# A selective-scan block on one Trainium2 core: GpSimd's products, sums and skip terms made two channel blocks at a time

## What is computed

```python
def step(h, inp):
    xt, dtt, bt, ct = inp
    dA = jnp.exp(A[None] * dtt[..., None])
    dB = dtt[..., None] * bt[:, None, :]
    h = dA * h + dB * xt[..., None]
    y = jnp.sum(h * ct[:, None, :], axis=-1)
    return (h, y)
...
xz = x @ w_in.T + b_in
x_ssm, z = jnp.split(xz, 2, axis=-1)
z = jax.nn.silu(z)
dt = jax.nn.softplus(x_ssm @ w_dt.T + b_dt)
Bm = x_ssm @ w_B.T + b_B
Cm = x_ssm @ w_C.T + b_C
y = _selective_scan(x_ssm, dt, A, Bm, Cm)
y = y + D[None, None, :] * x_ssm
y = y * z
y = y @ w_out.T + b_out
```

## Time and profile before

| what | value |
|---|---|
| time, median of 3 runs | 4594.26 us (4590.93 to 4594.27) |
| span of the profiled execution | 4588.9 us, 5.4 us less than that median |
| PE, busy | 4344.2 us, 95% |
| POOL, busy | 4161.1 us, 91% |
| ACT, busy | 3817.6 us, 83% |
| DVE, busy | 3679.8 us, 80% |
| POOL's products (L364), 2048 of 128 x 512 | 2590.8 us |
| POOL's sums (L375), 512 of 128 x 512 | 653.4 us |
| mean granted TensorE clock | 0.991 |

### The profile page before, as it was taken

One profiled execution on the slowest core, in us unless ns is written; L12 is line 12 of the kernel. 1 busy time (PEld: TensorE's weight loads), 2 busy tenths in 40 slices (PEclk: granted clock), 3 DMA queues, 4 the chain that ended last, 5 costly groups with the idle time before them and its releaser, 6 DMA issues. The chain is left out here.

```text
span 4588.9 us, 71982 instructions
## 1 busy us (share of the span) xinstructions
PE 4344.2 (95%) x22528; PEld 2805.6 (61%) x22528; DVE 3679.8 (80%) x5132; ACT 3817.6 (83%) x6371; POOL 4161.1 (91%) x3343
## 2 busy tenths in 40 slices
PE   7999999999999999999999999999999999999997
PEld 3666666666666666666666666666666666666664
DVE  3778888888887888888888888888878888888885
ACT  3788888888888888888888888888888888888885
POOL 3899999999999999999999999999999999999995
PEclk8999999999999999999999999999999999999999
DMA  3111111111111111111121111111111111111111
GB/s 129 45 43 58 58 58 45 56 51 57 60 58 48 49 59 59 58 46 54 51 62 59 59 44 56 51 57 60 54 45 54 60 61 58 47 53 51 58 49 39
DMA packets 140915, 254.79 MB, mean 56 GB/s; under 512 B 18597, under 2 KB 18597, under 8 KB 140538
## 3 DMA queue, kind: packets, MB, share of 16 engines
q1 hardware_dynamic: 140538, 250.19, 17.2%
HBM read 215.50 MB, written 34.63 MB: 55 GB/s over the span
## 5 line engine op out<-in xcount | busy, mean ns | idle before, releaser
L364 POOL TENSOR_TENSOR work<-work,c_bc 128x512 f32<-128x512 f32 x2048 | 2590.8, 1280 | 266.6 <-DVE work L1127 180.9
L1127 DVE TENSOR_TENSOR_SCAN work<-work,state,b_ps 128x512 f32<-128x512 f32 x1792 | 2250.5, 1273 | 351.9 <-PE b_ps L453 343.2
L839 ACT ACTIVATE work<-u_td,b_td 128x512 f32<-128x512 f32 x2048 | 1455.4, 711 | 147.5 <-PE b_ps L453 142.2
L829 ACT ACTIVATE work<-dt_t,neg_a 128x512 f32<-128x512 f32 x2048 | 1454.1, 710 | 12.5 <-DVE work L1127 12.1
L453 PE MATMUL b_ps<-ident,work 128*128 128x128 f32 x8192 | 1246.2, 275 | 67.2 <-DVE work L1127 57.0
L453 PEld LDWEIGHTS b_ps<-ident,work 128*128 128x128 f32 x8192 | 966.7, 142 | 344.5 <-issue 173.4
L530 PEld LDWEIGHTS y_ps<-ident,work 128*128 128x128 f32 x6144 | 758.4, 142 | 635.7 <-issue 586.5
L530 PE MATMUL y_ps<-ident,work 128*128 128x128 f32 x6144 | 916.2, 274 | 4.7 <-POOL work L375 3.5
L375 POOL TENSOR_TENSOR work<-work 128x512 f32<-128x512 f32 x512 | 653.4, 1276 | 40.2
L679 PE MATMUL dense<-h_t,w_in_t 128*128 128x512 f32 x1024 | 514.4, 599 | 9.2 <-DVE u_td L1210 8.9
L587 PE MATMUL dense<-w_out_t,proj 128*128 128x512 f32 x1024 | 508.6, 594 | 0.0
(11 more groups left out here) (115 smaller groups left out, 4523.0 us busy)
## 6 DMA issues: line engine op xcount, KB each, us to landing
c_bc<-c_d SPq DMA_DIRECT2D x512, 256.0 KB, 3.2
xn<-in_x SPq DMA_DIRECT2D x128, 256.0 KB, 5.1
x<-in_x SPq DMA_DIRECT2D x128, 256.0 KB, 4.4
out_dram<-x SPq DMA_DIRECT2D x128, 256.0 KB, 4.2
work<-in_wmod SPq DMA_DIRECT2D x2, 1024.0 KB, 6.3
w_in_t<-in_w_in_t SPq DMA_DIRECT2D x2, 1024.0 KB, 9.9
gain_shift<-par_d SPq DMA_DIRECT2D x8, 256.0 KB, 4.5
w_dt_t<-in_w_dt_t SPq DMA_DIRECT2D x1, 1024.0 KB, 11.3
```

The source lines that it names most:

```text
L364: gp.tensor_tensor(pr[:, (s * U + i) % PR_RING, :], hs[:, (s * U + i) % HS_RING, :], c_bc[:, (s * N + n) % C_RING, :], ALU.mult).then_inc( ...
L829: A(decay[:, (s * U + i) % DEC_RING, :], dt_t[:, s % 2, j, :], ACT.Exp, scale=neg_a[:, j, n:n + 1]).then_inc(S["dec_done"], 1)
L839: A(v[:, n % V_RING, tb, :], u_td[:, tb, :], ACT.Copy, scale=b_td[:, s % 2, tb, n:n + 1]).then_inc(S["v_done"], 1)
L1127: V.tensor_tensor_scan(hs[:, (s * U + i) % HS_RING, :], decay[:, (s * U + i) % DEC_RING, :], b_ps[:, i % 2, :], state[:, i:i + 1] if s % N ...
```

## The change

GpSimd takes units i and i + 1 (i even), which share the state and so C, with one instruction of 128 x 2 x 512 = 1024 columns. This goes for the product, the sum and the skip term: 42 instructions of 1024 columns in a step where 84 of 512 stood (32 products, 8 sums, 2 skip terms). C is read twice by a broadcast. The instruction stands where the second unit of the pair stood, and waits for the second unit's scan. Semaphores count pairs. The ring `pr` grows from nine to ten, so that a pair never wraps around; `hs` keeps its six places. The room comes from `w_cb`, whose weights were padded from 32 to 128 columns and now are not: the matmul of L653 writes 32 partitions in place of 128.

```diff
-    V_RING, DEC_RING, HS_RING, PR_RING, C_RING = 2, 6, 6, 9, 3
+    V_RING, DEC_RING, HS_RING, PR_RING, C_RING = 2, 6, 6, 10, 3
...
-    SKIP_AT = (8, 9, 10, 11)
+    SKIP_AT = (8, 10)
...
-        w_cb = sb("w_cb_t", [P, KD, P])
+        w_cb = sb("w_cb_t", [P, KD, 2 * N])
...
+            def both(ring, of, i):
+
+                return ring[:, i % of:i % of + 2, :]
+
             def product(s, i):
                 n, j = i // KD, i % KD
                 if j == 0:
                     gp.wait_ge(c_loaded[(s * N + n) % C_RING], ((s * N + n) // C_RING + 1) * Q)
-                gp.wait_ge(S["scan_done"], at("scan_done", s, i + 1))
+                gp.wait_ge(S["scan_done"], at("scan_done", s, i + 2))
...
-                gp.tensor_tensor(pr[:, (s * U + i) % PR_RING, :], hs[:, (s * U + i) % HS_RING, :],
-                                 c_bc[:, (s * N + n) % C_RING, :], ALU.mult).then_inc(S["prod_done"], 1)
+                made_here = both(pr, PR_RING, s * U + i)
+                gp.tensor_tensor(made_here, both(hs, HS_RING, s * U + i),
+                                 c_bc[:, (s * N + n) % C_RING:(s * N + n) % C_RING + 1, :].to_broadcast([P, 2, T]), ALU.mult
+                                 ).then_inc(S["prod_done"], 1)
...
-                gp.wait_ge(S["prod_done"], at("prod_done", s, i + 1))
-                gp.tensor_tensor(pr[:, (s * U + i) % PR_RING, :], pr[:, (s * U + i) % PR_RING, :],
-                                 pr[:, (s * U + i - KD) % PR_RING, :], ALU.add).then_inc(S["sum_done"], 1)
+                gp.wait_ge(S["prod_done"], at("prod_done", s, i // 2 + 1))
+                gp.tensor_tensor(both(pr, PR_RING, s * U + i), both(pr, PR_RING, s * U + i),
+                                 both(pr, PR_RING, s * U + i - KD), ALU.add).then_inc(S["sum_done"], 1)
...
                 for i in range(U):
-                    if has_s:
-                        product(s, i)
+                    if has_s and i % 2:
+                        product(s, i - 1)
                         if summed(i // KD):
-                            add_products(s, i)
+                            add_products(s, i - 1)
                     beside.until(i)
...
-                pe.wait_ge(S["prod_done"], at("prod_done", s, i + 1))
-                if i in SKIP_AT:
-                    pe.wait_ge(S["skip_added"], at("skip_added", s, j + 1))
+                pe.wait_ge(S["prod_done"], at("prod_done", s, i // 2 + 1))
+                if i - j % 2 in SKIP_AT:
+                    pe.wait_ge(S["skip_added"], at("skip_added", s, j // 2 + 1))
...
-                last = mm(long(s, "cb")[:, :], w_cb[:, k, :], xs_t[:, k, :], start=(k == 0), stop=(k == KD - 1))
+                last = mm(long(s, "cb")[0:2 * N, :], w_cb[:, k, :], xs_t[:, k, :], start=(k == 0), stop=(k == KD - 1))
...
-                    dve.wait_ge(S["prod_done"], at("prod_done", s, before + 1))
+                    dve.wait_ge(S["prod_done"], at("prod_done", s, before // 2 + 1))
```

More of the change, by code:

```diff
@@ L177, in build_program @@
             "SP": dict(stored_0=Q, stored_1=Q, stored_2=Q, stored_3=Q, c_stored=Q),
-            "Pool": dict(prod_done=U, skip_added=KD, sum_done=sums(U - 1), xsh_done=TB, x1_done=TB, dt_done=KD, u_done=KD, sz_done=KD),
+            "Pool": dict(prod_done=U // 2, skip_added=KD // 2, sum_done=sums(U - 1) // 2, xsh_done=TB, x1_done=TB, dt_done=KD, u_done=KD, sz_done=KD),
             "PE": dict(b_made=U, y_added=added(U - 1), s_ps=1, g_used=J, yz_ps=KD, out_ps=TB, res_used=TB, pre_ps=TB, xt_ps=KD, xs_ps=KD,
@@ L249, in _ @@
             load("wd_loaded", w_dt[:, :, :], blocks("w_dt_t"))
-            load("wd_loaded", w_cb[:, :, 0:2 * N], blocks("w_cb_t"))
+            load("wd_loaded", w_cb[:, :, :], blocks("w_cb_t"))
             load("wd_loaded", b_dt[:, :], ap["b_dt_c"])
@@ L294, in spread_c @@
                 if n >= C_RING:
-                    sp.wait_ge(S["prod_done"], at("prod_done", k, (n - C_RING) * KD + KD))
+                    sp.wait_ge(S["prod_done"], at("prod_done", k, (n - C_RING + 1) * KD // 2))
                 else:
-                    sp.wait_ge(S["prod_done"], at("prod_done", k - 1, (N + n - C_RING) * KD + KD))
+                    sp.wait_ge(S["prod_done"], at("prod_done", k - 1, (N + n - C_RING + 1) * KD // 2))
                 sp.dma_start(c_bc[:, (k * N + n) % C_RING, :], c_d[k % 2, n:n + 1, :].to_broadcast([P, T])
@@ L322, in step @@
                         sp.wait_ge(S["cb_done"], at("cb_done", f, 1))
-                        sp.wait_ge(S["prod_done"], at("prod_done", f - 2, U))
+                        sp.wait_ge(S["prod_done"], at("prod_done", f - 2, U // 2))
                         sp.dma_start(c_d[f % 2], cb_t[0:N, :]).then_inc(S["c_stored"], Q)
@@ L364, in product @@
-                gp.tensor_tensor(pr[:, (s * U + i) % PR_RING, :], hs[:, (s * U + i) % HS_RING, :],
-                                 c_bc[:, (s * N + n) % C_RING, :], ALU.mult).then_inc(S["prod_done"], 1)
+                for q in (r, r + 1):
+                    if q // KD in HELD:
+                        gp.wait_ge(S["sum_done"], at("sum_done", k, sums(q + KD) // 2))
+                    else:
+                        gp.wait_ge(S["y_added"], at("y_added", k, added(q)))
+                made_here = both(pr, PR_RING, s * U + i)
@@ L366, in product @@
+                gp.tensor_tensor(made_here, both(hs, HS_RING, s * U + i),
+                                 c_bc[:, (s * N + n) % C_RING:(s * N + n) % C_RING + 1, :].to_broadcast([P, 2, T]), ALU.mult
+                                 ).then_inc(S["prod_done"], 1)
                 if i in SKIP_AT:
-                    gp.wait_ge(S["prod_done"], at("prod_done", s, i + 1))
-                    gp.wait_ge(S["skip_done"], at("skip_done", s, j + 1))
-                    gp.tensor_tensor(pr[:, (s * U + i) % PR_RING, :], pr[:, (s * U + i) % PR_RING, :],
-                                     xs_t[:, j, :], ALU.add).then_inc(S["skip_added"], 1)
+                    gp.wait_ge(S["prod_done"], at("prod_done", s, i // 2 + 1))
+                    gp.wait_ge(S["skip_done"], at("skip_done", s, j + 2))
+                    gp.tensor_tensor(made_here, made_here, xs_t[:, j:j + 2, :], ALU.add).then_inc(S["skip_added"], 1)
@@ L524, in add_unit @@
                 if summed(i // KD):
-                    pe.wait_ge(S["sum_done"], at("sum_done", s, sums(i)))
-                pe.wait_ge(S["prod_done"], at("prod_done", s, i + 1))
-                if i in SKIP_AT:
-                    pe.wait_ge(S["skip_added"], at("skip_added", s, j + 1))
+                    pe.wait_ge(S["sum_done"], at("sum_done", s, (sums(i) + 1) // 2))
+                pe.wait_ge(S["prod_done"], at("prod_done", s, i // 2 + 1))
+                if i - j % 2 in SKIP_AT:
+                    pe.wait_ge(S["skip_added"], at("skip_added", s, j // 2 + 1))
                 for tb in range(TB):
@@ L949, in front @@
                     act.wait_ge(S["xs_ps"], at("xs_ps", f, m + 1))
-                    act.wait_ge(S["skip_added"], at("skip_added", s, m + 1))
+                    act.wait_ge(S["skip_added"], at("skip_added", s, m // 2 + 1))
                     A(xs_t[:, m, :], long(s, "xs", m)[:, :], ACT.Identity, bias=b_in[:, m:m + 1]
@@ L1120, in scan @@
                 if before >= 0:
-                    dve.wait_ge(S["prod_done"], at("prod_done", s, before + 1))
+                    dve.wait_ge(S["prod_done"], at("prod_done", s, before // 2 + 1))
                 else:
-                    dve.wait_ge(S["prod_done"], at("prod_done", s - 1, U + before + 1))
+                    dve.wait_ge(S["prod_done"], at("prod_done", s - 1, (U + before) // 2 + 1))
                 dve.wait_ge(S["state_done"], at("state_done", s, i // 2 + 1 - HS_RING // 2))
```

## The result

The changed kernel takes 4631.75 us (median of 4 runs, 4629.63 to 4632.31), the one before 4592.85 us on the same chip (4590.93 to 4594.27). The ratio is 1.0084, with a 95% interval of 1.0070 to 1.0098: slower, where 0.5% faster was forecast, and outside the range. A second measurement on another chip gave 1.0090 (1.0075 to 1.0105). The profiled span is 4630.5 us, 41.6 more than before.

A forecast was written before the change was run, and what follows sets the result against it. PE was taken as the bound, with POOL's queue on the path only at block 3's gate: 4588.9 - 55.2 (gate) + 33.2 (step's end) = 4566.9 us span, plus 5.4 gives a 4572 us median, 0.5% faster; range 4543 to 4612.

The forecast's parts named there:

- what bounds the kernel: PE, busy 133.6 of a step's 139.29 us; POOL, busy 129.8, counts only where PE or DVE waits for it.
- the price of a pair: One 1024-column GpSimd instruction was taken at 2.37 us, with 2.56 as upper bound and 2.28 as low end.
- the gain at the gate: Block 3's gate at unit 6: DVE's waiting multiplication starts 1.84 us earlier, 30 times, -55.2 us.
- the loss at the step's end: Pairs there make PE start unit 62 1.07 us later, unit 60's shorter wait contained; 31 times, +33.2 us.
- Hidden work costs nothing: The shorter w_cb matmul, scans' wait on the ring of six and the tenth place of `pr` were priced at nothing.
- Just in time: 0 at 2.37: Unit 30: POOL's pair work ends at 2247.32, PE wants it at 2247.38; no loss, 0.4 us at pair price 2.46.
- The first and last step ... aren't costed apart: The first and last step, where PE has less to do, got no separate cost.
- The 5.4 us from span to median: The median was taken to lie 5.4 us above the profiled span, turning 4566.9 into 4572 us.
- The rival "slower": A pair costs 2.46 us or more, so PE waits for units 60 and 62; 4600 to 4643, chance 0.25.
- the rings: Scans' wait on the ring of six and the tenth place of `pr` cost nothing, POOL being under four units behind.
- Nothing moves: Rival: PE is the bound, another DVE wait takes over, only 1.2 of 1.84 us stay; 4591 us, chance 0.17.
- the step's end is free: Rival: PE's wait for unit 62 is made up before the copies of y, only the gain remains; 4539, chance 0.1.

The follow-up runs named there:

- e1: The kernel before with only w_cb's weights narrowed to 32 columns, no pairs and no ring of ten: 4616.81 us, ratio 1.0060 to the kernel before.
- e2: The changed kernel with w_cb's matmul reading 128 columns of weights again, 96 of them unused neighbours: 4603.94 us, ratio 1.0032 to the kernel before.
- e6: The changed kernel with 128-column weights and DVE's small two-input instruction split into four tensor_scalar ones, all pairs kept: 4583.71 us, ratio 0.9987 to the kernel before.
- e10: The kernel before with w_cb's matmul using 64 of the 128 padded weight columns, nothing in memory moved: 4619.37 us, ratio 1.0063 to the kernel before.
- e4: The kernel before with the gate of block 3 at unit 5 in place of unit 6, no pairs: 4521.16 us, ratio 0.9853 to the kernel before.
- e3: The changed kernel with DVE's small two-input instruction made of four tensor_scalar ones (one tensor, one scalar column): 4610.89 us, ratio 1.0047 to the kernel before.
- e5: The changed kernel with units 56 to 63 taken singly, narrow weights kept: 4610.14 us, ratio 1.0046 to the kernel before.
- e8: The changed kernel with units 56 to 63 single, 128-column weights and DVE's small instruction as four tensor_scalar ones: 4558.60 us, ratio 0.9931 to the kernel before.
- e9: The kernel before with block 3's gate at unit 5, DVE's small instruction split, pairs only in units 12-27 and 32-55, ring of ten, 128-column weights: 4525.43 us, 0.9863.

## Why the prediction was wrong

**Right:** what bounds the kernel; the price of a pair (2.37 taken, 2.370 measured); the gain at the gate (1.84 a step forecast, 1.73 measured); the loss at the step's end (1.07 forecast for unit 62; measured 0.61 + 0.53 = 1.14, in two waits, of which the one for unit 60 is "contained" in the whole as forecast and makes the larger part). The estimate from the Trainium skill (GPSIMD Engine Reference, section 3.1: 4497 ns for 2048 columns) was 2.35; the measured value lies 0.02 above it.

**Wrong, first: "Hidden work costs nothing: the shorter w_cb matmul (the same 512 columns stream past it)".** I looked at what streams and not at the weights. It costs 0.84 a step, some 25 us of span (e1: 25.7). That is the largest single error, but it does not decide the sign alone: with wide weights the changed kernel is still slower (e2: 1.0032), and faster only when the second error is repaired too (e6: 0.9987). A weight load that before ran under the matmul ahead of it, and the one that follows, are no longer hidden. The rows show that at both changes of width; e1, e10 and e2 show that it is the width. The Trainium skill bears on it: TensorEngine Tiling (Array Packing), section Key Properties, says that changing the tiling mode drains the engine. The traces agree as far as they go: both loads at the change of width start only with their matmul (2295.57 and 2296.55). A drain as such they don't show, and that fewer than 128 columns select another mode I infer. A width between 64 and 128 was not tried.

**Wrong, second: "Just in time: 0 at 2.37" at unit 30.** 0.66 a step, some 20 us. The sum of durations was right: from scan 29's end at 2257.02 to the end of the sum (30, 31) at 2267.96 it is 10.94, and the forecast had 10.90. Scan 29 itself came late, since pairs change when POOL's instructions run and so how long DVE's small instruction ahead of that scan is held. I took scan times from the kernel before as if POOL's timing could not move them. The term had a margin of 0.06 us, which is none; it should have carried a range.

**Wrong, third: "The first and last step ... aren't costed apart".** They cost 14.7 us (0.4 + 8.5 + 5.8), 1.7 of them the narrow weights of steps 0 and 1 at 0.84 each. The 0.4 is scatter: a second execution of the same kernel starts step 0 some 1.1 us earlier than the kernel before, not 0.4 later. In step 0 the offset grows by 0.76 at unit 8, 0.89 at 11, 0.87 at 13 and 0.71 at 14. The first three are again DVE held by POOL. DVE has other work there, which runs once in the program:

```profile
93.79 1.75 DVE L1085 TENSOR_SCALAR tmp<-tmp 4x512 f32<-4x512 f32 x1
101.14 2.56 DVE L1081 TENSOR_SCALAR tmp<-tmp 4x512 f32<-4x512 f32 x1
```

while POOL runs

```profile
92.85 2.42 POOL L381 TENSOR_TENSOR work<-work 128x1024 f32<-128x1024 f32 x1
101.09 2.34 POOL L381 TENSOR_TENSOR work<-work 128x1024 f32<-128x1024 f32 x1
```

and before the two took

```profile
93.65 0.67 DVE L1079 TENSOR_SCALAR tmp<-tmp 4x512 f32<-4x512 f32 x1
99.93 0.47 DVE L1075 TENSOR_SCALAR tmp<-tmp 4x512 f32<-4x512 f32 x1
```

In the changed kernel both end some 0.3 us after the sum beside them. The ten instructions of this chain (L1079 to L1087, before L1073 to L1081) take 9.35 us in place of 7.70, which is the 0.76 + 0.89; scans 7 and 9 stand behind them. At unit 13 it is L1102 in the same way, 2.83 us in place of 1.75. At unit 2 of step 1 (2.00) PE waits 2.0 us for POOL's product at y_ps: that is the step's end, at a higher price. In the last step, too, PE waits for POOL at y_ps, but kernels without pairs also lose up to 3.0 us there against the kernel before (e1 2.9, e10 3.0), so not all of its 5.8 belongs to the pairs. Unit 14 stays open, and no run isolates any of these places; e2 and e6 have them too, since neither repair touches them.

The account, in spans: 4566.9 was forecast and 4630.5 measured, 63.6 apart. In each of 29 steady steps the gate gave 0.11 less, the end cost 0.07 more, unit 30 cost 0.66 and the weights 0.84, together 1.68, or 49. The steps outside make 14.7, of which the forecast had 0.3 (its 30th gate and its 30th and 31st step end). The sum agrees to within half a us, but the 14.7 is measured and only in part explained. The 5.4 us from span to median was too large as well: here the median lies 1.2 above the span, so the medians are 60 apart.

The rival "slower" was right in its sign and wrong in its cause: it rested on a pair price of 2.46 or more. I had no rival in which an edit priced at nothing cost something, though the weights, the rings and unit 30 all stood at nothing by argument alone. That this rival's range of 4600 to 4643 holds the measured time is luck. "Nothing moves" fell, since the gate's gain came nearly whole, and "the step's end is free" fell with the growth at units 1 and 2.

## What to carry to other kernels

When a wait for another engine's queue is what is to be won, first move the one instruction that is waited for: here one number in the order (e4) gives 68 us, while merging instructions frees 205 us of POOL that hardly anything was waiting for and makes each first unit of a pair late. Look at the edits that make room for a change as closely as at the change: taking weights from 128 to 32 columns cost 0.84 us a step and had been priced at nothing. A term that comes out "just in time" from the sums of another trace has a price between nothing and its whole chain, and wants both ends in the range; so do the steps in which the bounding engine has less to do.

## What the runs showed of the hardware

- Weights of 32 or 64 columns among weights of 128 cost PE 0.26 to 0.34 us each time that such a matmul group stands between wide ones, though the load is shorter. Padding to 128 columns, even with a neighbour's weights, avoids it (e2).
- A DVE instruction of 4 elements with two inputs in SBUF took 0.16 us when free and up to 1.34 in the changed kernel; in the 61 of 64 places there where it began under a running product of POOL it ended 0.02 to 0.03 us after that product. The same work by instructions with one tensor input and a scalar column took 0.57 for four, with no such wait (e3). One input alone is no safeguard: the TENSOR_SCALAR instructions of 512 columns in step 0 were held too (1.75 and 2.56 us; L1085 took 0.41 when nothing of POOL ran). The line over the whole changed program, with minimum, median and maximum in ns:

```profile
L1146 DVE SCALAR_TENSOR_TENSOR norm<-norm x64: 156/851/1340, 14.5 to 4599.0; 128x4 f32<-128x4 f32 x64
```

  and over the whole program before:

```profile
L1140 DVE SCALAR_TENSOR_TENSOR norm<-norm x64: 155/210/1567, 14.4 to 4559.4; 128x4 f32<-128x4 f32 x64
```

  The medians hide two places in a step. At unit 14 it takes some 0.66 us in both kernels. At unit 28 it takes 0.16 before and 1.14 after, since POOL's instruction is longer there. The 1.57 is a single place in the last step before, where a second product followed at once and DVE was held through it too. By the Trainium skill (SBUF — State Buffer, section "SBUF: two separate sides") a DVE operation with two SBUF inputs and a GpSimd operation that reads SBUF take the same port pair as an exclusive lock for a whole instruction; the trace agrees for the two-input instruction (0.02 to 0.03 us after the product's end in all 61 places).
- GpSimd's two-input operation takes 1.28 us for 512 columns and 2.37 for 1024, with a broadcast of C (L370) as without (L381: 2369 ns against 2370). By a straight line 0.19 of it does not grow with the columns, which is what a pair saves.
- A POOL instruction that waits for POOL's own one ahead starts 0.078 us after its end when that one adds one to the semaphore, and 0.143 us after when it adds two (e5, e8 and e9, medians). Within e5 the two differ in width as well; the changed kernel's pairs, as wide and adding one, have 0.078.
